# A fused transformer kernel on one core: the two ends of the first attention

## The reference, cut to what matters

```python
h, d_k = 16, 16
q = _proj_heads(_layernorm(x), q_proj_weight, h)      # and k, v in the same way
scores = jnp.einsum('bhqd,bhkd->bhqk', q, k) / sqrt(d_k) + mask       # causal
attn = jax.nn.softmax(scores, axis=-1)
out = jnp.einsum('bhqk,bhkd->bhqd', attn, v)
x = x + jnp.einsum('bsv,mv->bsm', out, o_proj_weight)
x = x + _L0_ffn_ref(_layernorm(x), ...)   # router over 8 experts, top 2, and a shared expert
# then a second attention with one head and a feed-forward part with ternary weights
```

## Time and profile before

| | |
|---|---|
| runs of the kernel before, us | 1741.65, 1742.82, 1743.44; median 1742.82 |
| profiled execution, us | 1740.07 |
| its span, first to last instruction, us | 1738.2 |
| TensorE (PE) busy | 1603.0 us, 92% |
| VectorE (DVE) busy | 951.1 us, 55% |
| ScalarE (ACT) busy | 946.1 us, 54% |
| GpSimd (POOL) busy | 447.5 us, 26% |
| mean granted clock of TensorE | 0.962 of full speed |

### The profile page before, as it was taken

One profiled execution on the slowest core, in us unless ns is written; L12 is line 12 of the kernel. 1 busy time (PEld: TensorE's weight loads), 2 busy tenths in 40 slices (PEclk: granted clock), 3 DMA queues, 4 the chain that ended last, 5 costly groups with the idle time before them and its releaser, 6 DMA issues. The chain is left out here.

```text
span 1738.2 us, 30810 instructions
## 1 busy us (share of the span) xinstructions
PE 1603.0 (92%) x10249; PEld 1104.6 (64%) x10250; DVE 951.1 (55%) x1846; ACT 946.1 (54%) x1521; POOL 447.5 (26%) x495
## 2 busy tenths in 40 slices
PE   6979999999999969999699999999579977997998
PEld 5833333333333338888578888888468966896887
DVE  6726656666545556887433333333366555655885
ACT  5679999999999944444222222222243434433432
POOL 0101121122121113556212222222333013001665
PEclk9989999999999989999899999999789988998999
DMA  7882856846723148224621111111402020000001
GB/s 239 224 227 87 197 151 140 211 137 141 164 38 67 24 154 308 95 70 152 233 68 51 51 49 53 49 48 52 139 26 73 1 73 1 1 1 4 25 24 49
DMA packets 88019, 169.40 MB, mean 97 GB/s; under 512 B 13504, under 2 KB 47808, under 8 KB 84768
## 3 DMA queue, kind: packets, MB, share of 16 engines
q1 hardware_dynamic: 80728, 146.90, 30.1%
q0 software_dynamic: 7056, 20.95, 3.7%
q10 hardware_dynamic: 128, 0.13, 0.1%
HBM read 96.67 MB, written 71.26 MB: 97 GB/s over the span
## 5 line engine op out<-in xcount | busy, mean ns | idle before, releaser
L836 ACT ACTIVATE probs<-ps_s 128x1024 f32<-128x1024 f32 (+3 forms) x640 | 511.9, 942 | 12.6 <-PE ps_s L902 9.9
L919 PE MATMUL ps_o<-probs,V 128*17 128x512 f32 (+3 forms) x2560 | 293.3, 536 | 2.3 <-POOL probs L824 1.7
L824 POOL TENSOR_SCALAR_AFFINE_SELECT probs<-probs 128x512 f32<-128x512 f32 x128 | 97.6, 770 | 428.2 <-ACT probs L836 426.9
L1645 DVE COPY slot_hT<-ps_hT 128x512 f32<-128x512 f32 x71 | 49.1, 691 | 196.4 <-PE ps_hT L1687 196.4
L902 PEld LDWEIGHTS ps_s<-Q_even,K_even 50*128 50x128 f32 x640 | 55.5, 187 | 133.3 <-ACT probs L836 119.6
L1695 PE MATMUL ps_slot_y<-we_out,slot_hT 128*128 x568 | 136.3, 383 | 2.2 <-issue 1.4
L2183 POOL TENSOR_TENSOR h_lo<-h,h_hi 128x512 fp32r<-128x512 f32 x64 | 89.5, 1417 | 178.4 <-DVE h L2229 178.4
L902 PEld LDWEIGHTS ps_s<-Q_odd,K_odd 50*128 50x128 f32 x640 | 54.7, 183 | 123.6 <-ACT probs L836 117.8
L902 PE MATMUL ps_s<-Q_even,K_even 50*128 50x512 f32 (+3 forms) x640 | 123.9, 445 | 9.1 <-DMA Q_even<-shift_parts 8.0
L902 PE MATMUL ps_s<-Q_odd,K_odd 50*128 50x512 f32 (+3 forms) x640 | 122.6, 438 | 0.6
L1606 POOL DMA_INDIRECT routed_rows<-slot_y,home_row x71 | 69.3, 977 | 175.1 <-ACT slot_y L1625 169.7
(11 more groups left out here) (274 smaller groups left out, 3933.1 us busy)
## 6 DMA issues: line engine op xcount, KB each, us to landing
weight_parts<-weight_hi SPq DMA_DIRECT2D x20, 512.0 KB, 4.4
weight_parts<-weight_lo SPq DMA_DIRECT2D x20, 512.0 KB, 5.1
we_hi<-weight_parts SPq DMA_DIRECT2D x19, 512.0 KB, 4.9
we_lo<-weight_parts SPq DMA_DIRECT2D x19, 512.0 KB, 7.3
slot_rows<-slots_in SPq DMA_DIRECT2D x71, 128.5 KB
qk_parts<-qk_hi SPq DMA_DIRECT2D x32, 256.0 KB, 4.8
qk_parts<-qk_lo SPq DMA_DIRECT2D x32, 256.0 KB, 5.7
we_hi<-attended_parts SPq DMA_DIRECT2D x16, 512.0 KB, 6.7
```

What stands on the lines that cost most here:

```text
L824: pool.affine_select(out=block_of, in_=block_of, compare_op=ALU.is_ge, fill=0.0, base=0, pattern=[[0, HG], [1, P]], channel_multiplier=-1) ...
L836: act.activation(probs[:, at % PROB_BUFS, 2 * p:2 * p + 2, off:BT], ps_s[:, s % SCORE_BUFS, :, off:BT], ACT.Exp).then_inc(exp_ok, 1)
L919: last = pe.matmul(ps_o[32 * h:32 * h + DH + 1, s % 2, off:BT], k["V"][:, group, SEQ_TILES * b + t, h, :], probs[:, at % PROB_BUFS, h, off ...
L1645: dve.tensor_copy(hT[:, :, :], ps_h[:, :, :]).then_inc(hT_ok, 1)
```

## The change

It has three parts.

1. The shifts of the first unit are loaded by POOL in `phase_qkv`, behind the stacks and the ones, and no longer by SP at the start of the attention. (In the branch of `phase_shift` that these inputs don't take, SP loads them again.)
2. The last of the 32 slices has its own chain. ACT makes the high part straight from PSUM, DVE the low part, and ACT copies the sums meanwhile. TensorE gathers the denominators with queries on the partitions, 128 x 16 in all, by eight matmuls that have four columns each. DVE copies them, takes the reciprocal of 16 columns, repeats each over 32 columns, and four transposes bring them back to 128 x 512. Then the product, the two parts and the stores follow as before.
3. The projection of the first block of rows is done by TensorE in the attention block, a fourth at a time between the links of that chain, into score banks that are no longer used. For this the score buffers are three tensors, of which two live on into `phase_tokens` as `ps_t` and `ps_y`. In `phase_tokens` the projection of block 0 is only a count.

```diff
@@ -357,7 +357,9 @@
                 load_ones(pool, io, k["first_stacks"][1], k["first_in"])
-                pool.wait_ge(k["first_in"], 16 * (STACK_LOADS + 2))
+                pool.wait_ge(zero_out, 16)
+                load_shift_rows(pool, io, 0, 0, k["first_stacks"][0], k["first_in"])
+                pool.wait_ge(k["first_in"], 16 * (STACK_LOADS + 2 + 2))
@@ -530,6 +532,14 @@
+def load_shift_rows(eng, io, g, b, Q, sem):
+    src = io["shift"].rearrange("m g b (p s) t -> s m (g b) p t", s=2)[:, :, BATCH * g + b]
+    for side in range(2):
+        at = HALF * side + STACK_ROWS
+        eng.dma_start(Q[at:at + SHIFT_PARTS].bitcast(F32), src[side]).then_inc(sem, 16)
 def load_stacks(eng, io, g, b, Q, K, sem):
@@ -581,7 +591,9 @@
                     load_stacks(sp, io, GROUPS - 1, 1, Q, K, loaded)
-                    sp.wait_ge(loaded, 16 * STACK_LOADS * UNITS)
+                    sp.wait_ge(stored, 16 * SHIFT_PARTS * UNITS)
+                    load_shift_rows(sp, io, 0, 0, k["first_stacks"][0], loaded)
+                    sp.wait_ge(loaded, 16 * (STACK_LOADS * UNITS + 2))
@@ -700,6 +712,7 @@
     SPREAD_AFTER = [5 if q == 0 else 3 for q in TURN]
+    LAST_BLOCK = SLICES * UNITS - 1
     LOADS = STACK_LOADS + 2
@@ -717,7 +730,8 @@
         pick = sb("denominator_pick", [P, HG, 32], F32R)
-        ps_s = mem.enter_context(nc.psum_tensor("ps_s", [P, SCORE_BUFS, 2, BT], F32))
+        ps_s = [k["ps_first"], k["ps_second"], mem.enter_context(nc.psum_tensor("ps_third", [P, 2, BT], F32))]
+        by_query, wide = sb("last_denominators", [P, TB, HG], F32), sb("last_inverse", [P, TB, HG, 32], F32)
         ps_o = mem.enter_context(nc.psum_tensor("ps_o", [P, 2, BT], F32))
@@ -748,18 +762,10 @@
-            def load_shifts(eng, u, j):
-
-                g, b = group_and_batch(u)
-                src = io["shift"].rearrange("m g b (p s) t -> s m (g b) p t", s=2)[:, :, BATCH * g + b]
-                for side in range(2):
-                    at = HALF * side + STACK_ROWS
-                    eng.dma_start(Q[j][at:at + SHIFT_PARTS].bitcast(F32), src[side]).then_inc(loaded[j], 16)
-
             def load(eng, u, j):
...
                 load_stacks(eng, io, g, b, Q[j], K[j], loaded[j])
-                load_shifts(eng, u, j)
+                load_shift_rows(eng, io, g, b, Q[j], loaded[j])
@@ -778,7 +784,6 @@
-                load_shifts(sp, 0, 0)
                 wait_parts(sp, k, BLOCKS)
@@ -834,7 +839,13 @@
                         act.activation(probs[:, at % PROB_BUFS, 2 * p:2 * p + 2, off:BT],
-                                       ps_s[:, s % SCORE_BUFS, :, off:BT], ACT.Exp).then_inc(exp_ok, 1)
+                                       ps_s[s % SCORE_BUFS][:, :, off:BT], ACT.Exp).then_inc(exp_ok, 1)
+                act.wait_ge(pv_ok, NT * UNITS)
+                act.wait_ge(picked_ok, LAST_BLOCK)
+                act.activation(sums_hi[:, :], ps_o[:, 1], ACT.Copy).then_inc(sums_ok, 1)
+                act.wait_ge(norm_ok, 4 * (LAST_BLOCK - 1))
+                act.wait_ge(sums_ok, 3 * LAST_BLOCK + 2)
+                act.activation(sums[:, 1], ps_o[:, 1], ACT.Copy).then_inc(sums_ok, 1)
                 act.wait_ge(result_ok, SLICES * UNITS)
@@ -842,7 +853,7 @@
                 dve.memset(ps_o[:, :, :], 0.0).then_inc(zero_ok, 1)
-                dve.sem_inc(loaded[0], 16 * STACK_LOADS)
+                dve.sem_inc(loaded[0], 16 * LOADS)
                 dve.wait_ge(pick_ok, 2)
@@ -855,12 +866,38 @@
+                def last_result():
+                    n, s = LAST_BLOCK, SLICES - 1
+                    dve.wait_ge(sums_ok, 3 * n + 1)
+                    dve.tensor_tensor(sums_lo[:, :], ps_o[:, s % 2], sums_hi[:, :].bitcast(F32), ALU.subtract
+                                      ).then_inc(sums_ok, 1)
+                    dve.wait_ge(picked_ok, n + 1)
+                    dve.tensor_copy(by_query[:, :, :].rearrange("p t h -> p (t h)"), ps_s[0][:, 0, 0:TB * HG]).then_inc(norm_ok, 1)
+                    dve.wait_ge(norm_ok, 4 * n + 1)
+                    dve.reciprocal(by_query[:, :, :], by_query[:, :, :]).then_inc(norm_ok, 1)
+                    dve.wait_ge(norm_ok, 4 * n + 2)
+                    dve.tensor_copy(wide[:, :, :, :], by_query[:, :, :].unsqueeze(3).to_broadcast([P, TB, HG, 32])
+                                    ).then_inc(norm_ok, 1)
+                    dve.wait_ge(picked_ok, n + 2)
+                    dve.wait_ge(sums_ok, 3 * n + 3)
+                    dve.tensor_tensor(result[:, :], sums[:, s % 2], ps_s[2][:, 0], ALU.mult).then_inc(norm_ok, 1)
+                    dve.wait_ge(norm_ok, 4 * n + 4)
+                    dve.wait_ge(stored[s % 2], 16 * ROWS_OUT * (n // 2))
+                    dve.tensor_copy(out_hi[:, s % 2], result[:, :]).then_inc(norm_ok, 1)
+                    dve.wait_ge(norm_ok, 4 * n + 5)
+                    dve.tensor_tensor(out_lo[:, s % 2], result[:, :], out_hi[:, s % 2].bitcast(F32), ALU.subtract
+                                      ).then_inc(result_ok, 1)
                 for u in range(UNITS):
...
                                 split_chunk(c)
+                        if n == LAST_BLOCK:
+                            last_result()
+                            continue
                         dve.wait_ge(pv_ok, NT * u + LAST[s] + 1)
@@ -899,7 +936,7 @@
                     for h in range(2):
-                        last = pe.matmul(ps_s[:, s % SCORE_BUFS, h, off:BT],
+                        last = pe.matmul(ps_s[s % SCORE_BUFS][:, h, off:BT],
                                          K[j][HALF * h:HALF * h + USED_ROWS, p, t * P:(t + 1) * P],
@@ -932,6 +969,32 @@
+                def project_rows(t):
+                    (hi, lo), (w_hi, w_lo) = ((front_rows(k, 0, n) for n in range(2)),
+                                              (projection(k, n).rearrange("p (c n) -> p c n", n=D) for n in range(2)))
+                    out = k["ps_second"][:, :, :].rearrange("p n (t d) -> p (n t) d", d=D)
+                    for d in range(DC):
+                        o = t * P
+                        mm3(pe, out[:, t], (hi[:, d, o:o + P], lo[:, d, o:o + P]), (w_hi[:, d], w_lo[:, d]), d == 0, d == DC - 1)
+                def last_denominators():
+                    pe.wait_ge(sums_ok, 3 * LAST_BLOCK + 2)
+                    for t in range(TB):
+                        at, out = slice(t * P, (t + 1) * P), ps_s[0][:, 0, HG * t:HG * t + HG]
+                        pe.matmul(out, sums_hi[:, at], pick[:, :, 0], start=True, stop=False)
+                        last = pe.matmul(out, sums_lo[:, at], pick[:, :, 0], start=False, stop=True)
+                    last.then_inc(picked_ok, 1)
+                def spread_inverse():
+                    pe.wait_ge(norm_ok, 4 * LAST_BLOCK + 3)
+                    for t in range(TB):
+                        last = pe.transpose(ps_s[2][:, 0, t * P:(t + 1) * P], wide[:, t].rearrange("p h r -> p (h r)"),
+                                            k["ident"][:, :])
+                    last.then_inc(picked_ok, 1)
                 scored = 0
@@ -941,8 +1004,16 @@
                         u, g = divmod(at - SPREAD_AFTER[s], NT)
-                        if u >= 0 and g == LAST[s]:
+                        if u >= 0 and g == LAST[s] and SLICES * u + s < LAST_BLOCK:
                             spread_denominators(u, s)
+                pe.wait_ge(exp_ok, 2 * len(STEPS))
+                pe.wait_ge(k["front_in"], 16 * FRONT_LOADS)
+                for t in (0, 1):
+                    project_rows(t)
+                last_denominators()
+                project_rows(2)
+                spread_inverse()
+                project_rows(3)
@@ -1060,7 +1131,8 @@
-        ps_t, ps_y = ps("ps_turned", [P, DC, BT]), ps("ps_rows", [P, TB, D])
+        ps_t = k["ps_first"][:, :, :]
+        ps_y = k["ps_second"][:, :, :].rearrange("p n (t d) -> p (n t) d", d=D)
         ps_m, ps_g = ps("ps_mid", [P, BT]), ps("ps_gated", [P, 2, BT])
@@ -1420,6 +1492,9 @@
                 def project(i, j, n):
+                    if is_first(i):
+                        pe.sem_inc(y_ok, 2)
+                        return
                     hi, lo = aT_hi[:, j], aT_lo[:, j]
@@ -2331,6 +2406,9 @@
             phase_shift(k)
+            banks = ExitStack()
+            k["ps_first"], k["ps_second"] = (
+                banks.enter_context(nc.psum_tensor(name, [P, 2, BT], F32)) for name in ("ps_first", "ps_second"))
             phase_attention(k)
@@ -2340,6 +2418,7 @@
             phase_tokens(k)
+            banks.close()
             phase_experts(k)
```

## The result

The changed kernel takes 1729.46 us (median of 11 runs, 1726.67 to 1735.51). The kernel before took 1741.65 us in 11 runs beside it (1734.89 to 1744.76). The ratio is 0.9938, 95% interval [0.9925, 0.9951]: 10.8 us less, with 8.5 to 13.1 as the ends.

What follows compares the result with a forecast made beforehand. It took TensorE, busy for 92% of the span, as the main engine, but idle or waiting in the three changed stretches. Gains of 2.6 + 3.6 + 1.3 = 7.5 us took the median 1742.82 to 1735.3 us, range 1732.0 to 1739.0.

Steps and rivals of the forecast that it cites:

- Part 1, 2.6 us: Start of the attention: TensorE begins once `ps_o` is clear, not when the shifts land; 2.6 us less, bounds 2.3 and 2.7.
- Part 2, 3.6 us: Last slice's chain at the attention's end: the stores begin 3.6 us earlier, 2.4 to 3.75 in single worse or better cases.
- ACT loaded no table: Last slice: a load of ACT's table for the copy was named as a sign that the forecast was wrong.
- half clock in the tail: Rival, chance 0.20: small matmuls in the tail and the token block's head run at half clock; 5.95 us less, 1736.9.
- Part 3, 1.3 us: Token block's start: DVE's two additions no longer wait for block 0's projection; 1.3 us less, bounds 0.85 and 1.5.
- TensorE is the engine that works through: Token block behind the first turn: TensorE works through and loads follow its counts, so the time won is kept.
- a warmer head: Rival, chance 0.10: clock stays full through the router and first shared expert matmuls; 1.7 to 3.5 us more gain.
- The sum: Whole kernel: 2.6 + 3.6 + 1.3 = 7.5 us less, for a median of 1735.3 us.
- The start did win: Rival, chance 0.08: something else holds TensorE at the attention's start, so the shifts win nothing; 4.9 us less, 1737.9.
- Nothing was given back: Rival, chance 0.08: token or expert blocks go by their own time; less than 3.5 us remain, 1739.3 or more.
- In the first unit a loss: Rival, chance 0.04: the clock rises later in the attention's first unit, making the kernel slower than before, 1746.5.
- The range: Whole kernel, for 8 in 10: 1732.0 to 1739.0 us, with 1 us for the runs.

Runs made afterwards that it cites:

- part 2 alone: Only the last slice's new chain put on the kernel before, block 0's projection left in the token block: 1737.68 us, ratio 0.9976.
- part 1 alone: Only the shifts' loading by POOL put on the kernel before: 1737.58 us, ratio 0.9982 to the kernel before.
- without the projection: The whole change with block 0's projection put back in the token block: 1733.90 us, ratio 0.9965 to the kernel before.
- busy_head: The whole change plus useless matmuls, 22 behind the projection's last fourth and 28 at the token block's start: 1730.99 us, ratio 0.9940 to the kernel before.
- both: The whole change plus the useless matmuls of busy_head and of busy_start: 1728.05 us, ratio 0.9933 to the kernel before.
- busy_start: The whole change plus 20 useless matmuls at three places ahead of the first scores: 1730.43 us, ratio 0.9940 to the kernel before.
- part 3 alone: Only block 0's projection moved behind the attention's last product, on the kernel before, old chain kept: 1738.54 us, ratio 0.9988.
- gap_filled: The whole change plus 16 useless matmuls between the token block's first turn and the router's matmuls: 1729.21 us, ratio 0.9928 to the kernel before.

## Why the prediction was right and where it was wrong

- *Part 1, 2.6 us.* Right: 3.55 us from clearing to first score in the mean before, 0.97 after, 2.58. The shifts were in at 87.1, forecast 86.8.
- *Part 2, 3.6 us.* Right: 3.8. From the end of the last product, as the forecast counted, it is 6.51 us and was to be 6.7. By term: gathering 1.06 (forecast 1.05), copy 0.17 (0.18), reciprocal 0.25 (0.26), repeat 0.43 (0.6, near the low end), transposes 0.66 (0.6). ACT loaded no table. That the projection's matmuls carry the clock through the tail was the reason given against the rival "half clock in the tail", and part 2 alone shows what that rival costs: 0.96 us in this chain. The matmuls of four columns, each with a load of 128 columns, start 0.11 us apart at full clock and 0.21 at half. The Trainium skill (TensorE: Matmul & The Clock Gate, LDWEIGHTS) gives a load's time as its columns over 1.2 GHz, 107 ns for 128, with no other figure for half clock. The trace agrees at full clock and disagrees at half.
- *Part 3, 1.3 us.* Right for the stretch it spoke of: 9.46 us in the mean before, 8.16 after. The 24 matmuls in the attention were free: the chain that they lie in is no longer than forecast.
- *The step that failed* is in part 3, behind the turn: "Behind it TensorE is the engine that works through", at the old speed. First turn to second turn took 23.09 us before and 21.15 after, in the mean, 1.94 less. The router's 16 matmuls fell from 3.41 to 1.78 us, and only 3.4 us of half clock followed them instead of 10.2 through both. This is the rival "a warmer head", with its size (1.7 to 3.5 more) and in the main its mechanism, to which I gave 0.10; the clock did fall again, only later and for less long. The row that could have told is the earlier trace rows with the earlier trace rows: the old kernel had 1.96 us of idle TensorE ahead of the turn and a second gap behind it, and the clock was already at half at 652.3. Without the projection's move the gain is gone (23.56), and with the second gap filled another 1.3 us come (19.65). Eight profiles have a gap of 1.45 to 1.96 us ahead of the turn and one of 2.10 behind it: three of before, part 1 alone, part 2 alone, without the projection, `busy_head` and both. In seven of them the clock was at half for the whole router, in the last it fell within it. Taking the first gap away is not enough by itself: in four profiles of the whole change the clock then held through the router, in `busy_start` and with part 3 alone it fell within it. In the four it had come back to full 0.7 to 1.6 us ahead of the turn, in the two only within it. That this decides is my reading; no run was made to test it, and why it came back sooner or later with the same code stays open.
- *The sum.* 2.6 + 3.8 + 1.3 + 1.9 = 9.6 us, against 10.8 and 10.6 measured, each with an interval of 2.3 to 2.7 to either side. The remaining 1 us lies within it. Mean time at half clock fell from 130.7 to 118.8 us a run, 11.9 us. The stretches at the hand-over hold 13.7 + 10.2 us of it in all three profiles of before and 6.8 + 3.4 in all four of after, 13.7 less, so nothing speaks for a gain of clock elsewhere. Whether the last us is real stays open. The 1.9 is a mean of profiles that agreed; `busy_start` says that some runs of the same hand-over may have much less of it.
- *The other rivals.* The start did win. Nothing was given back: third to eighth turn is 112.6 us in every profile. In the first unit a loss can't be excluded. The half clock there (13.7 or 17.1 us in both kernels) begins after the work of the block before, and the earlier first score puts more of the attention into it: about 11.4 us in the mean of four profiles against 8.7 of three. First score to last product took 522.5 us in the mean against 521.5, which is within the spread of the profiles; it runs from 520.0 us with 7.4 us of half clock behind the first score (part 1 alone) to 523.4 with 13.0 (`gap_filled`). So up to 1 us of part 1's 2.6 may have been given back.
- *The range.* It counted 1 us for the spread of runs, read off three runs that lay within 1.8 us. Twenty-nine runs of the same kernel lie within 10.9 us. The median of three, 1742.82, was itself 1.2 us above that of eleven. Without this the same sum would have said 1734.2.

No kernel tried beats the change clearly. `gap_filled` has the lowest ratio, 0.9928 against 0.9938, with intervals that overlap almost wholly.

## What to carry to other kernels

Where a chain of small steps hands work to and fro between TensorE and another engine, look for real matmuls of the next stage whose operands have already landed, and put them between the links: here they cost nothing, shortened the chain itself by 1.0 to 1.3 us through the clock (7.88 and 8.25 to 6.92) and, in four profiles against one, the stage behind it by 2.4 us (23.56 to 21.15). When costing such an edit, go on past the place it speaks of and ask of each stretch at half clock which idle time came ahead of it, and whether that idle time is still there. Useless matmuls are no substitute unless they fill the last gap ahead of the work that is to be fast: ahead of the turn they only opened an earlier gap, the clock fell ahead of the router, and the stretch cost 2.8 us more in that profile. Even the gap filled (19.65) showed no clear gain in the time. And before taking a stretch's time in a few profiles as the edit's doing, look at the same stretch in variants that leave it alone.

## What the runs showed of the hardware that was not expected

- TensorE can be busy almost without a break and remain at half clock: in the first unit for 9.4 to 13.1 us behind the first score, in four profiles of one program, and for 6.9 when useless matmuls ran ahead of it. In the kernel after, the second window below is busy for 6.00 of 6.00 us at 0.50:

```profile
104.00:108.00 4.00, 3.76 (x16) 0.98 (x16) 0.00 (x0) 3.88 (x5) 0.00 (x0) 0.50 0.77 216
108.00:114.00 6.00, 6.00 (x26) 1.33 (x28) 2.83 (x4) 3.88 (x4) 0.00 (x0) 0.50 1.14 180
114.00:121.00 7.00, 7.00 (x50) 1.97 (x49) 1.01 (x1) 6.38 (x8) 0.00 (x0) 0.97 0.97 160
```

- One program, four profiles: spans of 1725.4 to 1733.2 us. They differ mostly among the expert tiles (367.8 to 373.1 us from the first to the last), hundreds of us behind the edit, and ahead of the first score (at 101.44 to 103.78).
- DVE's copy with a source repeated 32 times took 0.43 us for 128 x 512, as long as its cast of that size without a repeat (`attention_hi` in the same profile), and its reciprocal of 128 x 16 took 0.25 us against 3.35 for 128 x 512.
